# Sixteen added semaphore waits on GpSimd, ScalarE and VectorE in a four-layer convolution kernel

## The chip, the cores and the metric

The kernel runs on one core of a Trainium2 chip. Its time is device time in microseconds of the whole program. TensorE, VectorE, ScalarE and GpSimd (PE, DVE, ACT and POOL in the rows) each work through an instruction list of their own, in order; SyncE (SP) issues DMAs. They are kept in step by semaphores alone.

## The reference

The input is x, 16 images of 64 x 64 positions with 256 channels, float32. Four layers follow, each adding to x what it computes of the group-normed x (32 groups):

```
x = x + L0(gn(x))   # nearest of 1024 codes for each position: scores against the codebook, argmin, gather of the code
x = x + L1(gn(x))   # row attention: f, g (32 channels) and h (256) of x; sigmoid(f g^T) over the 64 columns; times h
x = x + L2(gn(x))   # per image: softmax over 4096 x 4096 outer products x0*x1, summed with x2, sigmoid, gates gn(x)
x = x + L3(gn(x))   # linear attention, 4 heads of 32: softmax of q and of k, context, output projection, layernorm
```

## The kernel before

An image is held channel-major in SBUF (`XT`: 2 halves of 128 channels by 4096 positions), two images at a time. Work goes in 8 groups `g` of 512 positions, `u` counts 128 positions in a group, `t = 4g + u`. Most scratch tiles have two halves, chosen by `g % 2`, so that group g writes where group g - 2 was read.

The steps of a group are functions that exist under one name on each engine that takes part. Layer 0 is `l0_norm` (ACT normalizes into `n_x`, rounds to `n_hi`; POOL makes the rest `n_lo`), `score` (PE), `best` and `index` (DVE), `index` (POOL: an indirect DMA gathers the code rows into `quant`), `turn0` (PE) and `add0` (DVE). Layer 1 is `l1_norm` (ACT, then POOL), `l1_fg` and `l1_h` (PE, then ACT and DVE), `l1_scores` (PE), `l1_tanh` (ACT), `l1_out` (PE, DVE). Layer 2 is `fill` (PE), `exp` (ACT), `sums` (PE), with `bexp`/`bsum` beside it and `gated`/`gating`/`gated_add` at its end. Layer 3 is `l3_norm`, `l3_k`, `l3_kexp`, `l3_kturn`, `l3_ctx`, `l3_qv`, `l3_q` and so on, then `combine`, `final_sq` and `final_out`. `gn` in three parts makes the scale and shift of a group norm.

Three images are in work at once: for each k, layers 0 and 1 of image k (`new`), layers 2 and 3 of image k - 1 (`old`) and the output of image k - 2 (`last`). The order in which each engine runs the steps is written out by hand, one list for each engine, for the first image, for the 15 rounds of the loop, and for the last.

A `Step` is a semaphore with a count for each image. `after(im, i)` is the value at which item i of image im is done. `room(im, i, d)` is the value at which the item d places before i is done, so that its buffer is free; such semaphores begin with a credit of d. `wait_ge` calls stand ahead of an instruction, in the order of the code. An instruction carries one wait itself; the waits beyond it stand in `EVENT_SEMAPHORE` instructions ahead of it, which the engine's sequencer handles and which have the line number of a `wait_ge`. For instance `l1_norm` on ACT waits at line 576 (`l1_hed`) and at line 577 (`l1_xn`) before its activation at line 578, and the trace has 128 such events with line 577.

Of the kernel before, what the change touches and what calls it, by code (L numbers as in the profile page):

```python
# [16 lines left out]
GT = 4  # L17
# [69 lines left out]
def build(nc, x, emb, emb_t, wfg, bfg, wh, bh, w3, b3, wqv, wk, w_out, b_out, gamma, beta, ident_in, gmat_in, out):  # L87
# [6 lines left out]
    with ExitStack() as ctx:  # L94
# [6 lines left out]
        def step(name, per=NG, depth=0):  # L101
# [140 lines left out]
        mean_ready, mean_ps, var_ready, var_ps, ve_ready, pow_done, gn_ready = (  # L242
            [step(f"{n}{l}", 1) for l in range(4)]
            for n in ("mean_ready", "mean_ps", "var_ready", "var_ps", "ve_ready", "pow_done", "gn_ready"))

        l0_xn, l0_hi, l0_lo = step("l0_xn"), step("l0_hi"), step("l0_lo", NG, 2)
        l0_scored, l0_maxed, l0_indexed = step("l0_scored", 2 * NT, 16), step("l0_maxed", 2 * NT, 2), step("l0_indexed", NT, 2)
        l0_turned, l0_added = step("l0_turned", 2 * NG, 4), step("l0_added", 2 * NG, 1)

        l1_xn, l1_hi, l1_lo = step("l1_xn"), step("l1_hi"), step("l1_lo", NG, 2)  # L250
# [160 lines left out]
        def _(pool):  # L411
# [19 lines left out]
            def l0_norm(im, g, part):  # L431
                if part < 3:
                    return
                pool.wait_ge(*l0_hi.after(im, g))
                nc.gpsimd.tensor_tensor(n_lo[:, g % 2, :, :], n_x[:, g % 2, :, :], n_hi[:, g % 2, :, :],  # L435
                                        ALU.subtract).then_inc(l0_lo.sem, 1)

            def index(im, t):
                g, u = t // GT, t % GT
                pool.wait_ge(*l0_indexed.after(im, t))  # L440
                nc.gpsimd.indirect_dma_start(  # L441
                    quant[:, g % 2, u, :], None, emb_t,
                    bass.IndirectOffsetOnAxis(ap=idx[:, t % (2 * GT), 0:1], axis=0),
                ).then_inc(gathered[g % 2][u], 16)

            def l1_norm(im, g):
                pool.wait_ge(*l1_hi.after(im, g))
                nc.gpsimd.tensor_tensor(n_lo[:, g % 2, :, :], n_x[:, g % 2, :, :], n_hi[:, g % 2, :, :],  # L448
                                        ALU.subtract).then_inc(l1_lo.sem, 1)

# [3 lines left out]
                nc.gpsimd.tensor_tensor(here, here, gated[:, g % 2, :, :], ALU.add).then_inc(g_added.sem, 1)  # L454

            def l3_norm(im, g):
                pool.wait_ge(*l3_hi.after(im, g))
                nc.gpsimd.tensor_tensor(o_lo[:, g % 2, :, :], o_x[g % 2], o_hi[:, g % 2, :, :],
                                        ALU.subtract).then_inc(l3_lo.sem, 1)
# [77 lines left out]
        def _(act):  # L537
# [31 lines left out]
                    last.then_inc(l0_hi.sem, 1)  # L569

            def l1_norm(im, g):
                act.wait_ge(*gn_ready[1].after(im))
                for k in range(KC):
                    last = normed(n_x[:, g % 2, k, :], im, k, g, 1)
                last.then_inc(l1_xn.sem, 1)
                act.wait_ge(*l1_hed.room(im, 2 * g + 1, 4))
                act.wait_ge(*l1_xn.after(im, g))
                nc.scalar.activation(n_hi[:, g % 2, :, :], n_x[:, g % 2, :, :], copy).then_inc(l1_hi.sem, 1)  # L578

            def l1_fg(im, g):  # L580
                act.wait_ge(*l1_fged.after(im, g))
                if im + g == 0:
                    act.wait_ge(weights_in, 16 * NW)
                for j, kept in enumerate((FT, GTm)):
                    rr = slice(2 * CK * j, 2 * CK * (j + 1))
                    last = nc.scalar.activation(kept[:, g % 2, :], PS[rr, 4, 0:2 * P], copy, bias=fg_bias[rr, 0:1])
                last.then_inc(l1_fgkept.sem, 1)

            def l1_tanh(im, g):
                act.wait_ge(*l1_scored.after(im, g))  # L590
                nc.scalar.activation(tanhs[:, g % 2, :], PS[:, 4, 0:GT * ROW], ACT.Tanh, scale=0.5).then_inc(l1_tanhed.sem, 1)
                act.wait_ge(*l1_tanhed.after(im, g))
                for r in range(2):
                    rr = slice(r * ROW, (r + 1) * ROW)
                    last = nc.scalar.activation(attn[rr, g % 2, :, rr], tanhs[rr, g % 2, :].rearrange("p (u i) -> p u i", u=GT),
                                                copy, bias=ones[rr, 0:1])
                last.then_inc(l1_attn.sem, 1)
# [55 lines left out]
                last.then_inc(g_normed.sem, 1)  # L653

            def l3_norm(im, g):
                act.wait_ge(*gn_ready[3].after(im))
                for k in range(KC):
                    last = normed(o_x[g % 2][:, k, :], im, k, g, 3)
                last.then_inc(l3_xn.sem, 1)
                act.wait_ge(*l3_qved.room(im, g, 2))  # L660
                act.wait_ge(*l3_xn.after(im, g))
                nc.scalar.activation(o_hi[:, g % 2, :, :], o_x[g % 2], copy).then_inc(l3_hi.sem, 1)

            def l3_kexp(im, g):
                act.wait_ge(*l3_kneg.after(im, g))
                nc.scalar.activation(ke[:, g % 2, :, :].rearrange("p u n -> p (u n)"), bank(0), ACT.Exp,
                                     bias=kneg[:, g:g + 1], accum_out=ksum[:, g:g + 1]).then_inc(l3_kexped.sem, 1)
# [141 lines left out]
        def _(dve):  # L809
# [40 lines left out]
            def gn(im, layer, part):  # L850
                q, b = layer // 3, gn_bank(layer)
                if part == 0:
                    dve.wait_ge(*stats_done[layer].after(im, NG - 1))
                    for k in range(KC):
                        link(v.bn_aggr(mv[:, q, k, :], stats[:, layer, k, :, :].rearrange("p g n -> p (g n)")))
                    if layer < 2:
                        v.tensor_copy(dm[:, q, :], mv[:, q, :, 0]).then_inc(mean_ready[layer].sem, 1)
                    else:
                        v.tensor_tensor(dm[:, q, :], mv[:, q, :, 0], beta_c[:, :], ALU.subtract).then_inc(mean_ready[layer].sem, 1)
                if part == 1:  # L860
                    dve.wait_ge(*mean_ps[layer].after(im))
                    if layer < 2:
                        v.tensor_copy(gm[:, q, :], PS[:, b, 0:KC])
                    else:
                        v.tensor_tensor(gm[:, q, :], PS[:, b, 0:KC], beta_c[:, :], ALU.add)
                    link(v.tensor_tensor(dm[:, q, :], dm[:, q, :], PS[:, b, 0:KC], ALU.subtract))
                    link(v.tensor_tensor(vv[:, q, :], dm[:, q, :], dm[:, q, :], ALU.mult))
                    v.tensor_tensor(vv[:, q, :], vv[:, q, :], mv[:, q, :, 1], ALU.add).then_inc(var_ready[layer].sem, 1)
                if part == 2:
                    dve.wait_ge(*var_ps[layer].after(im))  # L870
                    v.tensor_scalar(ve[:, q, :], PS[:, b, 4:4 + KC], GN_EPS, None, ALU.add).then_inc(ve_ready[layer].sem, 1)
                    dve.wait_ge(*pow_done[layer].after(im))
                    v.scalar_tensor_tensor(out=gt[:, layer, :], in0=gm[:, q, :], scalar=-1.0, in1=gs[:, layer, :], op0=ALU.mult,  # L873
                                           op1=ALU.mult).then_inc(gn_ready[layer].sem, 1)
# [37 lines left out]
                stat(im, g, 1)  # L912

            def l1_h(im, g, w):
                dve.wait_ge(*l1_hed.after(im, 2 * g + w))
                v.tensor_tensor(H[:, g % 2, 2 * w:2 * w + 2, :], bank(6 - w).rearrange("p (u n) -> p u n", u=2),
                                h_bias[:, :].unsqueeze(1).broadcast_to([P, 2, C]), ALU.add).then_inc(l1_hkept.sem, 1)
# [101 lines left out]
                                ALU.mult).then_inc(l3_qsoft.sem, 1)  # L1019

            def l3_kturn(im, g):
                dve.wait_ge(*l3_kturned.after(im, g))
                v.tensor_copy(kt[:, g % 2, :, :], bank(5).rearrange("p (u n) -> p u n", u=GT)).then_inc(l3_kback.sem, 1)

# [69 lines left out]
            def final_out(im, c):  # L1094
                g = c // 2
                dve.wait_ge(*f_rstd.after(im, g))
                if c % 2 == 0 and im * NG + g >= 2:
                    dve.wait_ge(stored[g % 2], 16 * (im * NG // 2 + g // 2))
                dve.wait_ge(*f_turned.after(im, c))
                for u in range(2 * (c % 2), 2 * (c % 2) + 2):  # L1100
                    last = v.scalar_tensor_tensor(out=yout[:, g % 2, u, :], in0=Y[:, g % 2, u, :],
                                                  scalar=rstd[:, g % 2, 1, u:u + 1], in1=PS[:, back_bank(im, c), u % 2 * C:(u % 2 + 1) * C],
                                                  op0=ALU.mult, op1=ALU.add)
                last.then_inc(f_half.sem, 1)
# [632 lines left out]
```

## Time and profile before

| | us, or a count |
|---|---|
| median of 3 runs | 5468.85 (5467.99 to 5471.41) |
| the profiled execution | 5467.99 |
| its span, first to last instruction | 5466.2 |
| instructions in its trace, events among them | 109580 |
| PE busy | 5123.3 (94%) |
| DVE busy | 4387.4 (80%) |
| ACT busy | 4037.1 (74%) |
| POOL busy | 1964.2 (36%) |

The span is what the rows cover; the time has 1.8 us more around it. A round of the loop takes about 328 us. Busy times leave out what the sequencers handle, such as the events. A line number is one of the kernel before; the changed kernel has the same instructions at lines up to 17 higher.

### The profile page before, as it was taken

Reading aid. Unit: us, or ns where it says so; the run is one execution under the profiler, and the core shown is the slowest. Engines: PE = TensorE matmul, PEld = TensorE weight load, DVE = VectorE, ACT = ScalarE, POOL = GpSimd, SP = SyncE. Lnnn points to the kernel's source line nnn. Section 1 sums busy time; section 2 is a strip of 40 time slices with the busy share of each in tenths; the row PEclk is TensorE's granted clock in tenths of the full one; section 3 lists DMA queues with packets and bytes.
Section 4 is the critical chain, followed back from the end, with each engine's and each line's share of the span. In section 5 each row is a group of like instructions: output and inputs, shape, how many; then the busy total and the mean of one; then the engine's idle time right before and its main releaser. Section 6 shows DMA issues by size and latency. Waiting matters only on the chain.

```text
span 5466.2 us, 109580 instructions
## 1 busy us (share of the span) xinstructions
PE 5123.3 (94%) x42984; PEld 2689.9 (49%) x42984; DVE 4387.4 (80%) x9218; ACT 4037.1 (74%) x6279; POOL 1964.2 (36%) x1594
## 2 busy tenths in 40 slices
PE   7799999999999999999999999999999999999986
PEld 3436445363543646445363553645446464453624
DVE  8478797887878888797887978778798887978836
ACT  1477878678786877868778786787868778786785
POOL 4225143342423425143351423424244351433403
PEclk9899999999999999999999999999999999999988
DMA  2010201102021020211102021020211102011000
GB/s 76 29 37 12 75 27 57 42 7 81 20 71 32 25 65 14 74 29 44 52 8 80 22 67 36 21 66 17 71 32 37 56 11 77 26 62 38 12 31 32
DMA packets 167966, 227.84 MB, mean 42 GB/s; under 512 B 13793, under 2 KB 146657, under 8 KB 167457
## 3 DMA queue, kind: packets, MB, share of 16 engines
q1 hardware_dynamic: 142880, 153.70, 8.5%
q0 software_dynamic: 24576, 67.14, 4.2%
q8 instruction: 345, 5.65, 0.4%
q14 instruction: 165, 1.34, 0.1%
HBM read 153.55 MB, written 67.24 MB: 40 GB/s over the span
## 4 chain that ended last, share of the span: by engine, by line
PE 72%; DVE 13%; ACT 9%; issue 4%; DMA 1%; POOL 1%; DVEq 0%; SPq 0%; ACTq 0%; POOLq 0%
PE PS L1239 36%; PE PS L1416 14%; PE PS L1407 5%; PE PS L1350 3%; PE PS L1515 2%; PE PS L1273 2%; ACT big L618 2%; DVE work L896 2%; PE PS L1297 2%; DVE stats L878 2%; ACT n_x L551 2%; PE PS L1316 1%; DVE idx L902 1%; PE PS L1365 1%; ACT soft L618 1%
## 5 line engine op out<-in xcount | busy, mean ns | idle before, releaser
L618 ACT ACTIVATE big<-PS 128x1024 f32<-128x1024 f32 x1216 | 1207.5, 1028 | 384.7 <-PE PS L1407 350.8
L441 POOL DMA_INDIRECT quant_H<-emb_t,idx x512 | 509.0, 994 | 906.2 <-DVE idx L902 879.7
L1239 PE MATMUL PS<-e_hi,n_hi 128*128 128x512 f16 x2048 | 780.4, 381 | 16.5 <-DVE m L896 9.0
L1239 PE MATMUL PS<-e_lo,n_hi 128*128 128x512 f16 x2048 | 777.2, 379 | 0.0
L1239 PE MATMUL PS<-e_hi,n_lo 128*128 128x512 f16 x2048 | 777.2, 379 | 0.0
L618 ACT ACTIVATE soft<-PS 128x1024 f32<-128x1024 f32 x576 | 577.3, 1030 | 257.8 <-PE PS L1407 255.8
L1416 PE MATMUL PS<-big,w 128*4 128x512 f32 x4864 | 680.3, 646 | 0.0
L878 DVE BATCH_NORM_STATS2 stats<-XT 128x6 f32<-128x512 f32 x1024 | 652.9, 683 | 11.0 <-POOL XT L454 1.0
L902 DVE FIND_INDEX8 idx<-m,work 128x8 uint32<-128x1024 f32 x512 | 624.2, 1219 | 0.0
L1407 PE MATMUL PS<-rhs,lhs 12*128 12x512 bf16 x3584 | 522.8, 403 | 71.5 <-ACT big L618 35.6
L495 POOL TENSOR_TENSOR rstd<-rstd,mhalf 128x4 f32<-128x4 f32 x128 | 131.9, 1030 | 1123.1 <-DVE rstd L1091 1123.1
L896 DVE CUSTOM_DVE_ANT_0 work<-PS,e_bias 128x512 f32<-128x512 f32 x512 | 350.6, 685 | 163.7 <-PE PS L1239 162.5
L1407 PEld LDWEIGHTS PS<-rhs,lhs 12*128 12x128 bf16 x3584 | 126.8, 91 | 677.9 <-ACT big L618 242.2
L551 ACT ACTIVATE n_x<-XT,gt,gs 128x512 f32<-128x512 f32 x512 | 393.6, 806 | 72.9 <-DVE gt L873 70.5
L896 DVE CUSTOM_DVE_ANT_0 work<-PS,e_bias,m 128x512 f32<-128x512 f32 x512 | 379.4, 741 | 32.0 <-PE PS L1239 26.7
L1239 PE MATMUL PS<-qv_hi,o_both 128*128 128x256 f16 x2048 | 357.9, 273 | 21.6 <-DVE soft L1032 21.6
L1239 PEld LDWEIGHTS PS<-e_hi,n_hi 128*128 128x128 f16 x2048 | 199.4, 97 | 351.1 <-DVE m L896 123.8
L435 POOL TENSOR_TENSOR n_lo<-n_x,n_hi 128x1024 f16<-128x1024 f32 x128 | 273.6, 2137 | 259.3 <-ACT n_hi L567 258.2
L992 DVE CUSTOM_DVE_ANT_0 o_x<-o_x,o_both 128x1024 f32<-128x1024 f32 x256 | 311.5, 1217 | 61.8 <-ACT o_x L629 61.8
L454 POOL TENSOR_TENSOR XT<-XT,big 128x1024 f32<-128x1024 f32 x128 | 303.5, 2379 | 151.8 <-DVE big L999 149.9
L629 ACT ACTIVATE o_x<-o_both,negm,s 128x1024 f32<-128x1024 f32 x256 | 317.7, 1241 | 38.7 <-DVE bnum L992 38.7
L448 POOL TENSOR_TENSOR n_lo<-n_x,n_hi 128x1024 f16<-128x1024 f32 x128 | 273.4, 2136 | 160.7 <-ACT n_hi L578 160.7
(214 smaller groups left out, 11030.5 us busy)
## 6 DMA issues: line engine op xcount, KB each, us to landing
xin<-x SPq DMA_DIRECT2D x128, 512.0 KB, 4.3
out<-yout SPq DMA_DIRECT2D x128, 512.0 KB, 3.0
o_both<-rows_d SPq DMA_DIRECT2D x32, 512.0 KB, 7.1
quant_H<-emb_t,idx POOLq DMA_INDIRECT x512, 2.8
XT<-emb SPq DMA_DIRECT2D x1, 1024.0 KB, 6.1
rows_d<-n_hi SPq DMA_DIRECT2D x32, 4.0 KB
XT<-wh SPq DMA_DIRECT2D x1, 256.0 KB, 5.5
XT<-wqv SPq DMA_DIRECT2D x1, 256.0 KB, 5.6
```

The costliest lines, as they stand in the source:

```text
L441: nc.gpsimd.indirect_dma_start(quant[:, g % 2, u, :], None, emb_t, bass.IndirectOffsetOnAxis(ap=idx[:, t % (2 * GT), 0:1], axis=0),).then_ ...
L454: nc.gpsimd.tensor_tensor(here, here, gated[:, g % 2, :, :], ALU.add).then_inc(g_added.sem, 1)
L551: return nc.scalar.activation(dst, XT[:, im % 2, k, g, :], copy, scale=gs[:, layer, k:k + 1], bias=gt[:, layer, k:k + 1])
L618: nc.scalar.activation(E[h % 3][:, z * 1024:(z + 1) * 1024], bank(2 * z, 2), ACT.Exp).then_inc(exped.sem, 1)
L629: nc.scalar.activation(EB, x0_row, ACT.Exp, scale=s3[:, 1, t:t + 1], bias=negm[:, t:t + 1], accum_out=bden[:, i:i + 1]).then_inc(b_exped.s ...
L878: last = v.bn_stats(stats[:, layer, k, g, :], XT[:, im % 2, k, g, :])
L896: v.tensor_tensor_reduce(biased[:, t % 2, part], bank(5 + half), e_bias[:, part], 1.0, m8[:, t % 2, 0:1] if half else -BIG, ALU.add, ALU.m ...
L902: v.max_index(idx[:, t % (2 * GT), :], m8[:, t % 2, :], biased[:, t % 2, :]).then_inc(l0_indexed.sem, 1)
L992: v.tensor_tensor_reduce(EB, EB, x2_row, 1.0, 0.0, ALU.mult, ALU.add, bnum[:, i:i + 1]).then_inc(b_summed.sem, 1)
L1239: ins = mm(dst, a, b, start=first and j == 0, stop=last and j == 2)
L1407: ins = mm(bank(r), lhs[rr, t * P:(t + 1) * P], rhs[rr, f * GW:(f + 1) * GW], start=True, stop=True)
L1416: ins = mm(PS[32 * q:32 * q + 4, 4, :], w2[:, t, f, :], E[h % 3][:, q * 512:(q + 1) * 512], start=h == 0, stop=h == HALVES - 1, skip_group ...
```

## The change

Waits are added ahead of instructions that are there already: each names the last reader (or writer) of the buffer half that the instruction is about to overwrite (or read). No instruction other than waits is added, removed or moved.

```diff
@@ POOL
             def l0_norm(im, g, part):
+                pool.wait_ge(*l0_scored.room(im, 2 * (g * GT + GT) - 1, 4 * GT))
                 pool.wait_ge(*l0_hi.after(im, g))
             def index(im, t):
+                pool.wait_ge(*l0_turned.room(im, t // 2, 4))
                 pool.wait_ge(*l0_indexed.after(im, t))
             def l1_norm(im, g):
+                pool.wait_ge(*l1_hed.room(im, 2 * g + 1, 4))
                 pool.wait_ge(*l1_hi.after(im, g))
+                if g > 1:
+                    pool.wait_ge(*l1_fged.after(im, g - 2))
             def l3_norm(im, g):
+                pool.wait_ge(*l3_qved.room(im, g, 2))
                 pool.wait_ge(*l3_hi.after(im, g))
@@ ACT
             def l1_norm(im, g):
+                act.wait_ge(*l1_lo.room(im, g, 2))
                 act.wait_ge(*gn_ready[1].after(im))
 ...
                 act.wait_ge(*l1_hed.room(im, 2 * g + 1, 4))
+                if g > 1:
+                    act.wait_ge(*l1_fged.after(im, g - 2))
                 act.wait_ge(*l1_xn.after(im, g))
             def l1_fg(im, g):
+                act.wait_ge(*l1_scored.room(im, g, 2))
                 act.wait_ge(*l1_fged.after(im, g))
             def l1_tanh(im, g):
+                act.wait_ge(*l1_outed.room(im, 2 * g + 1, 4))
                 act.wait_ge(*l1_scored.after(im, g))
             def l3_norm(im, g):
+                act.wait_ge(*l3_lo.room(im, g, 2))
                 act.wait_ge(*gn_ready[3].after(im))
             def l3_kexp(im, g):
+                act.wait_ge(*l3_kturned.room(im, g, 2))
                 act.wait_ge(*l3_kneg.after(im, g))
@@ DVE
             def gn(im, layer, part):   # part 1
                     dve.wait_ge(*mean_ps[layer].after(im))
+                    dve.wait_ge(*mean_ready[layer].after(im))
             def l1_h(im, g, w):
+                dve.wait_ge(*l1_outed.room(im, 2 * g + 1, 4))
                 dve.wait_ge(*l1_hed.after(im, 2 * g + w))
             def l3_kturn(im, g):
+                dve.wait_ge(*l3_ctxed.room(im, g, 2))
                 dve.wait_ge(*l3_kturned.after(im, g))
             def final_out(im, c):
                 dve.wait_ge(*f_rstd.after(im, g))
+                dve.wait_ge(*f_y.after(im, c))
```

ScalarE in layer 1 of a round of the loop, before (L578 rounds to `n_hi`, L591 is the tanh of `l1_tanh`, L586 the first copy of `l1_fg`):

```order
L578 ACTIVATE n_hi<-n_x 128x1024 [waits l1_xn,l1_hed]
L591 ACTIVATE work<-PS 128x256 [waits l1_scored]
L595 ACTIVATE attn<-work,ones 64x4x64 [waits l1_tanhed]
L595 ACTIVATE attn<-work,ones 64x4x64
L551 ACTIVATE o_x<-XT,gt,gs 128x512 [waits g_gated]
L586 ACTIVATE work<-PS,fg_bias 64x256 [waits l1_fged]
L586 ACTIVATE work<-PS,fg_bias 64x256
L551 ACTIVATE n_x<-XT,gt,gs 128x512 [waits gn_ready1]
```

The same place now:

```order
L587 ACTIVATE n_hi<-n_x 128x1024 [waits l1_xn,l1_fged,l1_hed]
L602 ACTIVATE work<-PS 128x256 [waits l1_scored,l1_outed]
L606 ACTIVATE attn<-work,ones 64x4x64 [waits l1_tanhed]
L606 ACTIVATE attn<-work,ones 64x4x64
L557 ACTIVATE o_x<-XT,gt,gs 128x512 [waits g_gated]
L596 ACTIVATE work<-PS,fg_bias 64x256 [waits l1_fged,l1_scored]
L596 ACTIVATE work<-PS,fg_bias 64x256
L557 ACTIVATE n_x<-XT,gt,gs 128x512 [waits gn_ready1,l1_lo]
```

Nothing has moved; four of the five waiting instructions of the layer have one wait more. GpSimd at the start of layer 0 of a round, before:

```order
L428 TENSOR_TENSOR gs<-ve,mhalf 128x2 [waits ve_ready0]
L435 TENSOR_TENSOR n_lo<-n_x,n_hi 128x1024 [waits l0_hi] x2
L441 DMA quant_H<-emb_t,idx 128x256 [waits l0_indexed] x4
L435 TENSOR_TENSOR n_lo<-n_x,n_hi 128x1024 [waits l0_hi]
L441 DMA quant_H<-emb_t,idx 128x256 [waits l0_indexed] x6
```

The same place now:

```order
L428 TENSOR_TENSOR gs<-ve,mhalf 128x2 [waits ve_ready0]
L436 TENSOR_TENSOR n_lo<-n_x,n_hi 128x1024 [waits l0_hi,l0_scored] x2
L443 DMA quant_H<-emb_t,idx 128x256 [waits l0_indexed,l0_turned] x4
L436 TENSOR_TENSOR n_lo<-n_x,n_hi 128x1024 [waits l0_hi,l0_scored]
L443 DMA quant_H<-emb_t,idx 128x256 [waits l0_indexed,l0_turned] x6
```

Here too every step has kept its place, and the one wait of each has become two.

## Rows read from the trace of the kernel before

**Rows 1.** The page: shares of the chain that ended last.
```profile
PE 72%; DVE 13%; ACT 9%; issue 4%; DMA 1%; POOL 1%; DVEq 0%; SPq 0%; ACTq 0%; POOLq 0%
```

**Rows 2.** Stretches of one round: length, busy PE, PEld, DVE, ACT, POOL, clock, DMA.
```profile
774.00:834.00 60.00, 55.22 (x665) 41.44 (x665) 49.74 (x91) 52.88 (x82) 37.09 (x18) 0.97 0.01 4
1000.00:1104.00 104.00, 103.85 (x618) 42.73 (x620) 100.00 (x217) 63.33 (x81) 41.79 (x35) 1.00 0.13 38
```

**Rows 3.** Events by line: count, duration ns min/median/max, first and last start.
```profile
L577 ACTq EVENT_SEMAPHORE  x128: 17/17/17, 161.8 to 5114.5; - x128
L617 ACTq EVENT_SEMAPHORE  x15: 38/38/38, 569.1 to 5190.8; - x15
L998 DVEq EVENT_SEMAPHORE  x128: 49/50/514, 457.9 to 5359.3; - x128
```

**Rows 4.** Chain of waits in the last image: start us, us, what.
```profile
5374.27 0.07 issue
5374.34 2.13 POOL o_both L458
...
5383.04 0.02 issue
5383.06 0.02 ACTq L671
5383.08 0.04 issue
5383.12 0.61 ACT xin L672
5383.73 0.03 issue
5383.76 0.02 DVEq L1027
5383.78 0.04 issue
5383.82 0.70 DVE qmx L1030
```

**Rows 5.** Timeline of the set-up: start us, us, what, idle before it.
```profile
17.42 0.61 ACT L548 ACTIVATE h_hi<-XT 128x512 f16<-128x512 f32 x1
18.18 0.43 POOL L421 TENSOR_TENSOR fg_lo<-XT,fg_hi 128x128 f16<-128x128 f32 x1 [2.10 <-ACT h_hi L548]
```

**Rows 6.** Timeline of ScalarE in layer 2.
```profile
932.20 1.96 ACT L618 ACTIVATE soft<-PS 128x1024 f32<-128x1024 f32 x2
934.09 2.10 ACT L618 ACTIVATE big<-PS 128x1024 f32<-128x1024 f32 x2
```

**Rows 7.** Timeline of the entry to layer 1.
```profile
785.01 2.13 POOL L448 TENSOR_TENSOR n_lo<-n_x,n_hi 128x1024 f16<-128x1024 f32 x1 [2.97 <-ACT n_hi L578]
787.24 0.29 PE L1316 MATMUL PS<-n_hi,fg_hi 128*32 128x256 f16 x4 [0.83 <-issue]
```

**Rows 8.** Who waited for whom: us in total, times, longest us.
```profile
ACT soft L666 <- DVE kneg L1008: 101.6, 32, 4.3
ACT n_x L551 <- DVE gt L873: 70.5, 17, 39.0
PEld PS L1515 <- DVE yout L1101: 40.0, 66, 1.3
DVE quant_H L916 <- PE PS L1239: 34.3, 46, 9.2
ACT work L591 <- PE PS L1340: 28.9, 36, 3.1
ACT work L586 <- PE PS L1316: 17.5, 19, 1.3
```

**Rows 9.** Line 916, who waited for it (us, times).
```profile
  PE PS L1350: 4.5, 14
```

**Rows 10.** Line 1297, what ended its idle time (us, times).
```profile
  DMA quant_H<-emb_t,idx: 17.8, 27
```

## The prediction

> **What bounds the kernel now.** First the shares of the chain that ended last: the reader is to see PE with 72%, and the three engines that get new waits with 13%, 9% and 1% [rows 1]. So TensorE sets the time, and a delay elsewhere counts only where PE, or the engine that PE then waits for, stands still for it. Second, the stretches of a round: in layer 0 beside layer 2 (1000 to 1104 us) PE is busy for 103.85 of 104.00 us, so that nearly every new stall of PE lengthens the program; where layer 1 stands beside the end of layer 2 (774 to 834 us) PE is busy for 55.22 and ACT for 52.88 of 60.00 us [rows 2], so the two hand the chain to each other. Third, the list of who waited for whom, which shows how often an instruction that gets a new wait now starts late, released by another engine [rows 8].
>
> **Do the new waits block?** Each names work that has already ended when the older wait passes, because every engine runs in order. POOL's `l0_norm` waits for scores that ACT has waited for before the `n_hi` that POOL reads. `index` waits for a `turn0` whose sum DVE's list has (`add0(t // 2 - 4)`) ahead of `index(t)`. ACT's `l1_tanh` waits for `l1_out(g - 2)`, which PE's list has ahead of `l1_scores(g)`; the same is true of `l1_h(g)`, of `l3_k(g)` after `l3_kturn(g - 2)` and of `l3_kturn(g)` after `l3_ctx(g - 2)`. `l1_lo` and `l3_lo` of group g - 2 were waited for by the PE work that ACT's older steps wait for. `f_y` and `mean_ready` are DVE's own, and the answers of POOL and PE that DVE waits for come after them. So nothing is held until a later moment than today, and no transfer is triggered earlier or later but by the small delays below. What is left is the price of the wait instruction itself.
>
> **What is added.** An instruction carries its first wait, and an event takes up to two more. By the code's order the older wait, the one that comes last in time, stands behind the new one in 11 of the 16 places and is pushed into the event, while the instruction keeps the new one, long satisfied. On POOL one wait becomes two or three for `l0_norm`, `l1_norm`, `l3_norm` at 128 each and for `index` at 512: 896 events. ACT gets 128 x 5 less 1 = 639 (`l1_norm`'s first, `l1_fg`, `l1_tanh`, `l3_norm`, `l3_kexp`; one `l1_fg` has an event already). DVE gets 64 (`gn`) + 256 (`l1_h`) + 128 (`l3_kturn`) + 126 (`final_out`, where a store is waited for) = 574. In `gn` the late wait stays on the instruction. Elsewhere an event grows from one wait to two: ACT's `n_hi` of line 578 96 times, `final_out` 130 times.
>
> **The price of one.** Where the event holds the late wait, the chain shows 0.02 us until the event starts, 0.02 for it and 0.04 until ACT's instruction starts; for DVE 0.03, 0.02 and 0.04 [rows 4]. The delay over a wait that the instruction carries is the last two, 0.06 us on ACT; for DVE I take 0.07, since these are rounded. On POOL a carried wait starts 0.07 us after the release [rows 4]; in the set-up, with an event, POOL's line 421 starts at 18.18 after ACT ended at 17.42 + 0.61 = 18.03, which is 0.15 [rows 5]: 0.08 more. An event with two waits takes 38 ns on ACT against 17, and on DVE 50 [rows 3] against 0.02 us [rows 4]: 0.02 and 0.03 more. Where the event's waits are satisfied while the instruction before still runs, it costs nothing: the first of two exponentials at 934.09 has an event (line 615) and starts before the pair ahead of it has ended at 932.20 + 1.96 = 934.16 [rows 6].
>
> **The sum**, over the places where a release comes late and PE stands behind it:
> - Entry to layer 1. PE idles 0.83 us and starts at 787.24, 0.10 after POOL's `n_lo` ended (785.01 + 2.13) [rows 7]; that hangs on ACT's L551, released late by `gt` 17 times [rows 8]. ACT 0.06 + POOL 0.08 = 0.14, in 16 images: 2.2 us. Queued behind the waiting instructions are ACT's next norm and POOL's next `n_lo`, which shift alike.
> - Middle of layer 1: L591 was released late by PE 36 times [rows 8]. Between nothing (PE has other work) and 36 x 0.06 = 2.2; I take one per round, 15 x 0.06 = 0.9, since ACT is busy for most of the stretch and its events are passed early. L586 was late 19 times and L666 32 times [rows 8], 1.1 and 1.9 at most; I take nothing, as PE has other steps queued between.
> - `l1_h`: DVE was late 46 times [rows 8], and PE waited for it 14 times [rows 9]: 14 x 0.07 = 1.0, between nothing and 3.2.
> - Gathers: PE waited for a gather 27 times [rows 10]. Each is issued 0.08 us later: 27 x 0.08 = 2.2. The trace has no gather behind an event, so this may be anything from nothing to twice that, 4.3. Queued behind each on POOL are the next gathers and `n_lo`; POOL is busy for 41.79 of 104 us there [rows 2].
> - Events with two waits: line 577 waits for ACT's own instruction just before and is always late, 96 x 0.02 = 1.9; about half stands on the path, 1.0. `final_out`: PE's loads waited for L1101 66 times [rows 8], half of them of the kind that grows: 33 x 0.03 = 1.0, at most 130 x 0.03 = 3.9.
> - Layer 3 is entered behind other PE work but in the last image: 0.1. `gn` and `l3_kturn`: nothing.
>
> 2.2 + 0.9 + 1.0 + 2.2 + 1.0 + 1.0 + 0.1 = 8.4 us. The profiled execution took 5467.99, so 5476.4; it lies 0.9 below the median of the runs, so 5477.3, or 0.15% more. The floor is no delay at all. The ceiling has every late release on the path: ACT 104 x 0.06 = 6.2, DVE 3.2, POOL 16 x 0.08 + 4.3 = 5.6, double waits 1.9 + 3.9, together 20.8: 5489.7. Below nothing there is no bound to set, since no wait is taken away and no order changes.
>
> **Rivals.**
> - *Absorbed* (5466 to 5472). The 0.06 to 0.08 us pass into idle time that a later wait would have had anyway. For it: PE has some 5 us of idle time in the 60 us of layer 1 [rows 2]. Against it: in layer 0 PE has 0.15 us of it in 104.
> - *Satisfied events cost too, slower* (5490 and more). The place is ACT in layer 1: 8 groups with 3 new events each, 24 in a round. If the sequencer could not pass them under the instruction before, each would cost the 0.06 of a late one: 15 x 24 x 0.06 = 21.6 us, and the time would be 5468.9 + 21.6 + 8.4 = 5498.9; it decides from about one in two of them exposed. Against it: the exponentials with an event start without a gap [rows 6]. The Trainium skill, Advanced Engine Details and Errata, section Network/Comms, gives 50 to 100 ns for a sequencer to read a semaphore's value; paid at each of these 360 events, that would be an estimated 18 to 36 us. By that rule alone this rival would be the likeliest; the trace agrees with its size only for late releases, and shows it hidden otherwise.
> - *One of the waits does block.* If ACT's norm of group g had to stay behind POOL's queue, each time it could cost one `n_lo`, 2.13 us [rows 7]; once a round gives 15 x 2.13 = 32 us, 5501. The orders of the lists speak against it.
>
> **How the numbers follow.** Two runs of this kernel can be told apart from about 0.2%, 10.9 us, so slower means above 5479.8 and faster below 5457.9. The forecast has 0.66: its own range is 5472 to 5488, of which 0.17 lies above 5479.8. Absorbed 0.22, satisfied events 0.07, a blocking wait 0.03. For a gain nothing speaks but a luckier meeting of queues, 0.02. So faster 0.02, same 0.49 + 0.22 = 0.71, slower 0.17 + 0.07 + 0.03 = 0.27. The range 5467 to 5488 leaves out the two dear cases and little more.
>
> **What would show it.** The trace has 109580 instructions and should have 2109 more, all events. In each image the first ACT norm of layer 1 should start 0.06 us later after `gt`, the first `n_lo` 0.15 after `n_hi` in place of 0.07, and PE's idle time before L1316 should grow by 0.14. Busy times of the engines should stay within 0.1%; layer 2 up to the start of the next layer 0, where only `final_out` has a new wait, should keep its length. The forecast is wrong if ACT shows gaps of 0.06 us between instructions that nobody releases late, if POOL's gathers move by more than 0.1 us, or if a new wait's semaphore comes after the older one. The Trainium skill, Perfetto Trace Analysis, section DVE / Act Engine Instruction, says that the sequencer is free for the next instruction once it has pushed one into the wait queue, whereas one that only the sequencer handles holds it until its wait is over: what is queued behind a late event is then decoded late as well. By that, short instructions behind a late event would show gaps too; no row here prices that.

## The result: 0.78% slower, outside the range

| | before | after |
|---|---|---|
| median of the runs, us | 5470.13 (5467.99 to 5473.2) | 5508.83 (5506.09 to 5519.77) |
| profiled execution, us (span) | 5467.99 (5466.2) | 5509.96 (5508.2) |
| mean granted clock in it | 0.963 | 0.957 |
| instructions in the trace | 109580 | 111689 |

The ratio is 1.0078, interval 1.0062 to 1.0092. I had 5477.3 and a range up to 5488. The 2109 additional events are there to the one. The time is not where my sum looked for it.

### The profile page after: what moved, and what is told of

It is laid out like the page before. It is cut to its first block, busy times and chain, and to the rows that moved or that the text cites. A ratio compares the mean times of both kernels' runs of the same rounds, so it can differ in the third digit from the quotient of the medians.

```text
span 5508.2 us, 111689 instructions
## 1 busy us (share of the span) xinstructions
PE 5155.3 (94%) x42984; PEld 2694.4 (49%) x42984; DVE 4393.6 (80%) x9218; ACT 4042.8 (73%) x6279; POOL 1977.0 (36%) x1594
## 4 chain that ended last, share of the span: by engine, by line
PE 72%; DVE 12%; ACT 7%; issue 5%; DMA 1%; POOL 1%; DVEq 0%; SPq 0%; ACTq 0%; POOLq 0%
PE PS L1256 36%; PE PS L1433 13%; PE PS L1424 6%; PE PS L1367 3%; PE PS L1532 2%; DVE work L910 2%; PE PS L1290 2%; ACT big L629 2%; PE PS L1314 2%; DVE idx L916 1%; DMA quant_H<-emb_t,idx 1%; PE PS L1333 1%; ACT n_x L557 1%; DVE stats L892 1%; PE PS L1382 1%
## 5 line engine op out<-in xcount | busy, mean ns | idle before, releaser
L443 POOL DMA_INDIRECT quant_H<-emb_t,idx x512 | 521.6, 1019 | 929.0 <-DVE idx L916 768.4
L436 POOL TENSOR_TENSOR n_lo<-n_x,n_hi 128x1024 f16<-128x1024 f32 x128 | 273.6, 2137 | 240.9 <-ACT n_hi L573 188.0
L1433 PE MATMUL PS<-soft,w 128*4 128x512 f32 x2304 | 336.0, 658 | 0.0
```

The costliest lines, as they stand in the source:

```text
L443: nc.gpsimd.indirect_dma_start(quant[:, g % 2, u, :], None, emb_t, bass.IndirectOffsetOnAxis(ap=idx[:, t % (2 * GT), 0:1], axis=0),).then_ ...
L1433: ins = mm(PS[32 * q:32 * q + 4, 4, :], w2[:, t, f, :], E[h % 3][:, q * 512:(q + 1) * 512], start=h == 0, stop=h == HALVES - 1, skip_group ...
```

## The profile after

The page first: busy time of the engines after, and the shares of its chain.

```profile
PE 5155.3 (94%) x42984; PEld 2694.4 (49%) x42984; DVE 4393.6 (80%) x9218; ACT 4042.8 (73%) x6279; POOL 1977.0 (36%) x1594
PE 72%; DVE 12%; ACT 7%; issue 5%; DMA 1%; POOL 1%; DVEq 0%; SPq 0%; ACTq 0%; POOLq 0%
```

The line of before that answers to the first:

```profile
PE 5123.3 (94%) x42984; PEld 2689.9 (49%) x42984; DVE 4387.4 (80%) x9218; ACT 4037.1 (74%) x6279; POOL 1964.2 (36%) x1594
```

The shares hardly differ from [rows 1], and DVE, ACT and POOL are busy for 6, 6 and 13 us more. PE runs the same 42984 matmuls and is busy for 32.0 us more, while its idle time grows from 5466.2 - 5123.3 = 342.9 to 352.9, by 10.0. So of the 42 us 10 are more waiting and 32 are the same matmuls taking longer, and the clock does most of that. A mean clock of 0.957 means 2 x (1 - 0.957) x 5508 = 474 us at the lower of the two levels (1.2 GHz), against 2 x 0.037 x 5466 = 404 before. The trace's own list of clock stretches says 473.8 and 404.3, and PE is busy in 82 to 84% of them. At half speed PE works 0.41 us longer in each us of them: 69.5 x 0.41 = 28 of the 32.

That is not yet what the clock costs the program, because a slower PE also waits less for the others. The net price shows where one kernel is run many times, as its half clock differs from run to run. The 55 executions of the kernel before beside the experiments have between 382 and 483 us of it, and take 0.26 us more for each us more. Over all 153 executions listed for the 14 kernels, each set about its own mean, it is 0.28 (0.26 to 0.31). At 0.28 the 69.5 us are worth 19 of the 42, and some 23 are delay. Against the mean of before in the first group of experiments, the eight executions of after are 36 us longer with 45 us more half clock: 12.5 for the clock and 23.4 for delay.

**The waiting** is at the gathers. First after, then before: a search of codes on DVE and the gather on POOL that it releases (start us, us, what, idle before).

```profile
739.65 1.22 DVE L916 FIND_INDEX8 idx<-m,work 128x8 uint32<-128x1024 f32 x1
741.64 0.95 POOL L443 DMA_INDIRECT quant_H<-emb_t,idx  x1 [3.55 <-DVE idx L916]
```

```profile
743.14 1.22 DVE L902 FIND_INDEX8 idx<-m,work 128x8 uint32<-128x1024 f32 x1
744.63 0.95 POOL L441 DMA_INDIRECT quant_H<-emb_t,idx  x1 [3.05 <-DVE idx L902]
```

The search ends at 740.87 and the gather starts 0.77 us later; before, 744.36 and 0.27. By the semaphore events of the whole trace it is 762 ns (407 gathers within 10 ns of it) against 259 (424). The event itself is short (count, ns min/median/max, first and last start):

```profile
L442 POOLq EVENT_SEMAPHORE  x512: 17/17/17, 49.0 to 5097.6; - x171
```

On a tensor_tensor of POOL a late event adds 65 ns (68 to 133), by the same semaphore events. A gather behind one loses 0.50 us, over seven times as much. I read the rest as preparation of the gather that runs under the wait when the gather carries it, and starts only afterwards when an event ahead of it waits; no row shows that preparation by itself. In the chain after, that half us stands as "issue" between the search and the DMA:

```profile
767.97 1.31 DVE idx L916 x2
769.32 0.72 issue
770.04 2.75 DMA quant_H<-emb_t,idx
772.79 0.04 issue
772.83 0.45 PE PS L1314 x2
```

Who waited for it, from the list of waits after (us, times, longest), and under it what ended the idle time before line 1314, which answers to [rows 10]:

```profile
PEld PS L1314 <- DMA quant_H<-emb_t,idx: 23.5, 28, 2.6
PE PS L1314 <- DMA quant_H<-emb_t,idx: 16.6, 21, 2.2
```

```profile
  DMA quant_H<-emb_t,idx: 40.2, 49
```

The first of the two lists before:

```profile
PEld PS L1297 <- DMA quant_H<-emb_t,idx: 11.9, 20, 2.2
PE PS L1297 <- DMA quant_H<-emb_t,idx: 6.0, 7, 2.0
```

The 27 waits of [rows 10] were 20 of weight loads, which run beside the matmuls, and 7 of PE itself. Now PE waits 21 times, for 16.6 us in place of 6.0: 10.6 us. That its whole idle time grew by 10.0 is chance: in the trace of the first kernel below these waits grow by 9.9 us and the idle time by 2.7, since other waits shrink.

**Does the new wait block?** The profile names PE's line 1314 as the releaser of 23 gathers after, for 53.7 us, which looks like it. The semaphore events say no: for every one of the 512 gathers `l0_turned` had its value before `l0_indexed` did, the closest by 15 us. A gather carries the new, satisfied wait, and the page reads its releaser from there.

**The rest of my list.** The entry to layer 1 after:

```profile
779.16 0.16 DVE L887 SCALAR_TENSOR_TENSOR gt<-gm,gs 128x2 f32<-128x2 f32 x1 [0.84 <-POOL gs L428]
779.41 1.52 ACT L557 ACTIVATE n_x<-XT,gt,gs 128x512 f32<-128x512 f32 x2 [0.99 <-DVE gt L887]
781.02 1.06 ACT L587 ACTIVATE n_hi<-n_x 128x1024 f16<-128x1024 f32 x1
782.22 2.13 POOL L453 TENSOR_TENSOR n_lo<-n_x,n_hi 128x1024 f16<-128x1024 f32 x1 [3.10 <-ACT n_hi L587]
```

0.09 us behind `gt` and 0.14 behind `n_hi`, as forecast. What ended PE's idle time before the line of the first products of layer 1 (us, times) was this before

```profile
  issue: 33.6, 74
  ACT work L591: 30.3, 76
  POOL n_lo L448: 6.3, 1
```

and is this after:

```profile
  ACT work L602: 35.8, 76
  issue: 29.6, 71
  POOL n_lo L453: 6.7, 1
```

Together 70.2 us and 72.1, over all groups of the layer. Ahead of the first product of each image, where my sum had 2.2 us, it did not grow: 13.4 us over the 16 images before, with none at all in five of them, and 11.6 after. The start is later, but the wait it should lengthen is not there every time. The waits at other edited steps hardly moved (to compare with [rows 8]), and all 256 events of `final_out` now take the 50 ns of a double one [rows 3]:

```profile
ACT soft L679 <- DVE kneg L1023: 103.9, 32, 4.7
PEld PS L1532 <- DVE yout L1118: 40.7, 66, 1.3
DVE quant_H L931 <- PE PS L1256: 36.7, 51, 9.4
ACT work L602 <- PE PS L1357: 30.3, 36, 3.1
```

```profile
L1116 DVEq EVENT_SEMAPHORE  x256: 49/50/50, 584.4 to 5500.8; - x128
```

**The clock.** Stretches at the entry to layer 2 (length, busy PE, PEld, DVE, ACT, POOL, clock, DMA): after,

```profile
892.00:896.00 4.00, 2.53 (x47) 1.42 (x45) 3.83 (x8) 3.26 (x6) 0.00 (x0) 1.00 0.00 0
896.00:903.00 7.00, 6.79 (x64) 1.88 (x62) 4.43 (x18) 5.21 (x8) 0.00 (x0) 0.51 0.36 102
```

and the same place before:

```profile
893.00:897.00 4.00, 2.57 (x49) 1.67 (x46) 3.87 (x7) 2.91 (x6) 0.00 (x0) 1.00 0.00 0
897.00:904.00 7.00, 6.14 (x74) 1.84 (x76) 4.99 (x21) 7.00 (x10) 0.00 (x0) 1.00 0.41 132
```

Both have PE busy for only some 2.55 of 4 us, for two pauses of 0.7 us each. After it the clock is at half for 7 us in the one, at full in the other, and PE gets through 64 matmuls in place of 74. Such a pause doesn't always bring the fall, but in both traces each round has three places where it can: the entry to layer 2, `gn` of layer 0 and `gn` of layer 1. Half clock by place in rounds 1 to 14, us, from the trace's list:

| | entry to layer 2 | gn 0 | gn 1 | first and last image |
|---|---|---|---|---|
| before | 68 | 102 | 68 | 165 |
| after | 102 | 116 | 79 | 177 |

The windows of [rows 2] show it too. Layer 1 has 0.94 for 0.97, and in layer 0 PE waits 1.1 us for two gathers, where it waited for none:

```profile
1000.00:1104.00 104.00, 102.90 (x606) 42.51 (x602) 98.73 (x216) 62.62 (x81) 42.58 (x35) 1.00 0.14 39
774.00:834.00 60.00, 55.27 (x664) 41.78 (x661) 48.31 (x88) 52.52 (x82) 37.11 (x18) 0.94 0.01 2
```

## The experiments

Each is compared with runs of the kernel before on its own chip. Clock is the mean over the runs; half clock is 2 x (1 - clock) x time; the next column, called the delay below, is the mean time less 0.28 of it, against the same for before, with the standard error of the kernel's own mean. For the kernels with matmuls, which have some 240 us less of half clock, it hangs on that price: their own executions give 0.34, which would add 14 us. What they differ by among themselves hardly depends on it. The ratios, with their 95% intervals, differ a little from those of the medians (1.0048 and 1.0049 for the first two); differences in us below are of means unless they are said to be of medians. PE's waits for gathers, us, are from the list of waits of the profiled run.

| kernel | median, us | ratio, interval | clock | half clock | delay: time less 0.28 of it, against before | PE waits for gathers |
|---|---|---|---|---|---|---|
| before, beside the next four | 5474.9 | | 0.9603 | 435 | 0 +- 0.5 | 6.0 |
| gather's wait alone | 5501.1 | 1.0040 (1.0025 to 1.0055) | 0.9567 | 477 | +12.8 +- 1.7 | 15.9 |
| all but it | 5501.8 | 1.0041 (1.0026 to 1.0057) | 0.9563 | 480 | +12.2 +- 0.7 | 3.7 |
| gather's wait behind | 5480.0 | 1.0004 (0.9994 to 1.0015) | 0.9602 | 436 | +1.6 +- 0.5 | 4.2 |
| all waits behind | 5485.0 | 1.0012 (1.0002 to 1.0022) | 0.9586 | 454 | +2.7 +- 0.6 | 3.6 |
| before, beside the next four | 5474.5 | | 0.9603 | 435 | 0 +- 0.6 | |
| late waits first | 5472.1 | 0.9992 (0.9983 to 1.0001) | 0.9594 | 445 | -6.2 +- 0.4 | |
| layer 3's waits alone | 5484.9 | 1.0014 (1.0004 to 1.0023) | 0.9590 | 450 | +4.7 +- 0.8 | |
| before with matmuls | 5436.9 | 0.9924 (0.9911 to 0.9938) | 0.9822 | 194 | +29.5 +- 1.0 | 4.6 |
| after with matmuls | 5457.0 | 0.9963 (0.9949 to 0.9976) | 0.9832 | 183 | +52.3 +- 0.5 | 16.4 |
| before, beside the last four | 5478.3 | | 0.9599 | 439 | 0 +- 0.8 | |
| matmuls, late waits first | 5420.0 | 0.9901 (0.9883 to 0.9919) | 0.9832 | 182 | +18.0 +- 1.1 | |
| half the matmuls, late first | 5442.9 | 0.9932 (0.9912 to 0.9951) | 0.9760 | 261 | +13.2 +- 1.6 | |
| matmuls and gather's wait | 5448.6 | 0.9948 (0.9933 to 0.9964) | 0.9817 | 200 | +39.8 +- 1.2 | 17.1 |
| matmuls at layer 2 alone | 5447.8 | 0.9943 (0.9930 to 0.9955) | 0.9698 | 329 | -0.3 +- 0.8 | |

The expectations were written with 0.41 as the price of a us at half clock. At that price kernels 1, 2 and 5 have delays of +7.4, +6.2 and -7.5 us, and these are the figures that the later expectations start from.

**1. The gather's wait alone.**

```
 def index(im, t):
     g, u = t // GT, t % GT
+    pool.wait_ge(*l0_turned.room(im, t // 2, 4))
     pool.wait_ge(*l0_indexed.after(im, t))
```

> The kernel before with one new wait alone: index waits for the room of l0_turned ahead of its own l0_indexed, so that the late wait sits in an event and the gather carries the satisfied one. Theory G (an indirect gather starts 0.26 us after a release that it carries and 0.76 behind a late event, and the 0.50 us are exposed in layer 0): most of the 39 us, so 5495 to 5505 us, with the gathers at 0.76 again. Rival R (the rest of the waits, 0.06 to 0.11 us at each late release on ACT, DVE and POOL, make the loss): within 10 us of before, 5470 to 5480, though the gathers start at 0.76. Rival C (any disturbance of PE's rhythm costs through stretches at the lower clock): something between, with PE's stretches at half clock as long as in the changed kernel (472 us, before 403).

The median lies in G's 5495 to 5505, but before is at 5474.9 here. The edit costs 25 us (26 by medians), neither G's most of 39 nor under R's 10. Its gathers start 762 ns after their release, PE waits 15.9 us for them, and 12.8 us are delay. 42 us more of half clock make the other 12, so C is in it.

**2. All but it.**

```
 def index(im, t):
     g, u = t // GT, t % GT
-    pool.wait_ge(*l0_turned.room(im, t // 2, 4))
     pool.wait_ge(*l0_indexed.after(im, t))
```

> The changed kernel without index's new wait: 1597 of the 2109 new events stay. Theory G: what my sum had without the gathers, 6 us, so 5474 to 5480 us, and gathers at 0.26 us after their release. Rival R: 5495 to 5508, since the waits that it blames are all in. Rival C: more than 5485 with stretches at half clock near 472 us.

G's 5474 to 5480 is missed by 22 us, and G as the whole story falls; R's range is met here and C's condition too. The delay is 12.2 us, twice what my sum had without the gathers (8.4 - 2.2 = 6.2); the clock adds 46 x 0.28 = 13. The two halves together give 0.40 + 0.41 = 0.81% for the whole's 0.78%. Their delays add up, 12.8 + 12.2 = 25.0 for the whole's 23.4; their half clock doesn't, 42 + 46 us for 45.

**3 and 4. The same events behind the late wait.** In 3 the two waits of `index` change places; in 4 the same is done in all 11 steps where a new wait stood first, as here:

```
 def l1_fg(im, g):
-    act.wait_ge(*l1_scored.room(im, g, 2))
     act.wait_ge(*l1_fged.after(im, g))
+    act.wait_ge(*l1_scored.room(im, g, 2))
```

> As the first of these, but the new wait stands behind l0_indexed: 512 new events all the same, each now with the satisfied wait, while the gather carries the late one. Theory G: 0 to 3 us over before (5469 to 5473 us), gathers at 0.26 us. Rival S (an event costs its time wherever it stands): as slow as the first one, 5495 or more. Rival C: over 5480.

> The changed kernel with the same 2109 events, but in each of the 11 steps where the older wait stood behind a new one the older stands first, so that the instruction carries the wait that comes late. Theory G and the small delays of late events alike: 0 to 4 us over before (5469 to 5474 us), with releases to starts as before (ACT 23 ns, DVE 24, POOL 68, gathers 260). Rival S: 5500 or more. Rival C: over 5480.

Delays of 1.6 and 2.7 us: 512 or 2109 satisfied events cost next to nothing (S falls). The fourth still has the events with two waits, for which my sum had 2.0 us. The late wait on the instruction gives the old latencies back (ACT 23 ns, DVE 24, POOL 68, gathers 259), and PE waits 4.2 and 3.6 us for gathers. So nearly all of the delay, and most of the loss, is the order of two lines in each step. The fourth still has 0.0017 less clock, worth 5 us, and lies 8 us over before (10 by medians): my 0 to 4 us was too low, and C's bound of 5480 was passed.

**5. Late waits first, in before.** Five old steps get the same treatment, the largest being `best`:

```
 def best(im, t, half):
     part = slice(half * 512, (half + 1) * 512)
+    dve.wait_ge(*l0_scored.after(im, 2 * t + half))
     if half == 0:
         dve.wait_ge(*l0_indexed.room(im, t, 2))
     else:
         dve.wait_ge(*l0_maxed.after(im, 2 * t))
-    dve.wait_ge(*l0_scored.after(im, 2 * t + half))
```

> The kernel before with no new wait: in five steps that already had two or three (best, gating, final_sq, final_out on DVE, l3_qv on ACT) the one that comes late stands first, so that the instruction carries it. Releases that cost 94 to 133 ns before should cost 24. Theory K (a late release that PE stands behind costs its delay and then, through longer pauses, more time at the lower clock): 5 to 25 us faster than before, with a granted clock above 0.961. Rival D (only the delay counts, and DVE's are off PE's path): within 3 us of before. Rival S (an order of waits is worth nothing): no change and releases as before.

The releases that took 94 to 133 ns take 24, but for the second half of `best`, whose wait for its own first half now stands in the event (134 ns). The delay falls by 6.2 us. The clock takes 3 of it back (its trace has 137 us of half clock at the entry to layer 2, before 68), and the interval reaches 1.0001. The time alone, 2 us less by medians, would also suit D. K's sign for the clock is wrong here: shorter delays did not raise it.

**6 and 7. PE kept busy in the pauses.** The edit is cut to its lines with `keep`; in the first round, which has no `last`, the first of them has no wait.

```
+def keep(im, n, b, *done):
+    if done:
+        pe.wait_ge(*done)
+    for _ in range(n):
+        mm(PS[:, b, 256:384], ident16[:, :], ident16[:, :], start=True, stop=True)
...
-fill(old, 30, 1); gn(new, 0, 1); fill(old, 31, 0)
-gn(new, 0, 2); fill(old, 31, 1)
+keep(last, 5, 5, *f_y.after(last, 2 * NG - 1))
+fill(old, 30, 1); keep(old, 4, 5); gn(new, 0, 1); fill(old, 31, 0)
+keep(old, 5, 5); gn(new, 0, 2); fill(old, 31, 1)
...
-fill(old, 55, 0); gn(new, 1, 1); fill(old, 55, 1); gn(new, 1, 2)
-sums(old, 53); sums(old, 54); sums(old, 55); gate_chain(old, 0); l1_fg(new, 0)
+keep(new, 14, 5, *l0_maxed.after(new, 2 * NT - 2))
+fill(old, 55, 0); keep(new, 4, 5); gn(new, 1, 1); fill(old, 55, 1); keep(new, 5, 5); gn(new, 1, 2)
+sums(old, 53); sums(old, 54); sums(old, 55); keep(new, 9, 5); gate_chain(old, 0)
+keep(new, 11, 5); l1_fg(new, 0)
...
+keep(new, 9, 7, *pieces_kept[1].after(new, 1))
```

> The kernel before with 57 additional matmuls of 128 columns in each round (some 3.4 us of PE work at full clock), in the places where PE stands idle ahead of the stretches at half clock: around gn of layers 0 and 1, ahead of the first products of layer 1, and ahead of layer 2. They write a free bank and nobody reads them. Theory K (the stretches at half clock follow from these pauses, and each us of them costs about 0.4): fewer of them, 250 to 350 us in place of some 430, and 20 to 70 us faster. Rival P (the clock doesn't hang on these pauses, or the matmuls come late and delay the work behind them): half clock as before, and 0 to 50 us slower.

> The changed kernel with the same additional matmuls in the same places. Theory K: two thirds of its loss is clock, so it comes within 15 us of the kernel before with these matmuls, what is left being the delays of 13 us. Rival D (the loss is all delay): it stays 38 us above the kernel before with these matmuls. Rival P: above 5508.

The count in the first expectation is wrong: there are 66 in a round, 990 in all. PE is busy with them for 79.1 us, 0.08 us each and not the 0.1 of the later expectations. They take 241 us of half clock away, more than K had. At 0.28 that is worth 68 us, against some 30 that the matmuls add, and the kernel is 38 us faster than before. Its mean clock, and under it the windows of the entry to layer 2 and, in two rows, of `gn` of layer 0:

```profile
core 0: 5437.6 us, clock 0.982
```

```profile
890.00:900.00 10.00, 8.99 (x126) 3.30 (x120) 7.38 (x26) 9.62 (x13) 0.00 (x0) 1.00 0.43 140
965.00:975.00 10.00, 9.16 (x74) 3.28 (x74) 6.75 (x19) 9.66 (x13) 0.69 (x1) 1.00 0.16 54
975.00:985.00 10.00, 8.44 (x58) 2.62 (x55) 2.99 (x8) 9.46 (x14) 2.13 (x1) 1.00 0.00 0
```

`gn` of layer 0 in before, where the clock falls:

```profile
970.00:980.00 10.00, 8.44 (x55) 2.74 (x58) 6.71 (x19) 9.49 (x13) 0.70 (x1) 0.91 0.16 54
980.00:990.00 10.00, 10.00 (x58) 2.34 (x51) 2.28 (x6) 8.90 (x12) 2.14 (x1) 0.75 0.00 0
```

The change costs 20 us with the clock held in both, and 36 to 39 without. K's "within 15" is missed by 5, because its two thirds of clock rest on the price of 0.41. The delay between the two is 52.3 - 29.5 = 22.8 us, as large as without the matmuls (23.4): the delay is the larger part of the loss, and the matmuls take away the clock's part.

**8. Layer 3's waits alone.**

```
+pool.wait_ge(*l3_qved.room(im, g, 2))      # l3_norm, ahead of l3_hi
+act.wait_ge(*l3_lo.room(im, g, 2))         # l3_norm, ahead of gn_ready[3]
+act.wait_ge(*l3_kturned.room(im, g, 2))    # l3_kexp, ahead of l3_kneg
+dve.wait_ge(*l3_ctxed.room(im, g, 2))      # l3_kturn, ahead of l3_kturned
```

> The kernel before with the new waits of layer 3 alone: l3_norm on POOL and ACT, l3_kexp, l3_kturn (512 events). My sum had 0.1 us for them. Theory K: they delay the end of layer 3, where PE's pauses stand ahead of layer 2, so the stretches at half clock that start there (7 of 15 rounds before, 11 after) come in more rounds: 5 to 15 us slower, nearly all of it clock. Rival L (the entry to layer 1 and l1_h carry what the gathers don't): within 3 us of before.

0.14% slower, 8.8 us: 4.7 of delay, and 4 for 15 us more of half clock, so not "nearly all" clock; in its trace the entry to layer 2 has 109 us of it in 12 rounds (before 68 in 8). L falls, and so does my 0.1 us for layer 3.

**9 to 12. What the matmuls hold, and where.** The first is 5 and 6 together; the second has 35 of the 66 matmuls; the third is 6 with the edit of 1; the fourth has only the last line of the edit of 6.

> The kernel before with both: the late waits first, and all 66 additional matmuls in each round (990 in all; 66, not 57 as I wrote for the first kernel with them, some 0.1 us each in its trace). Alone, the order of the waits took 7.5 us from the time without the clock's share and gave most of it back in clock. Theory K: with the clock held by the matmuls the 7 us stay, so 5428 to 5434 us, 5 to 9 below the kernel with the matmuls alone. Rival D (nothing is gained from the order in either case): 5434 to 5440.

> As the one above with 35 of the 66 matmuls in each round, in the same nine places. They save 31 x 15 x 0.1 = 47 us of PE work, of which a third or so lay in PE's waits anyway. Theory K: where the shorter ones still keep the clock up it gains up to 25 us on the full set (5405 to 5430); where a pause is left too long the clock falls there again, and it lands between 5430 and 5450. Told apart by the half clock in the trace: under 250 us or over 300.

> The kernel before with the 66 matmuls and index's new wait alone ahead of l0_indexed. Without the matmuls that wait cost 7 us of delay and 17 us of clock. Theory K: the clock's share is gone, the delay stays: 5 to 15 us over the kernel with the matmuls (5442 to 5452). Rival D (delay of gathers is all of it): 24 us or more over it, 5461 or more.

> The kernel before with the 9 matmuls ahead of layer 2 alone, and none around gn. Theory K says place by place: the stretches at half clock that start at the entry to layer 2 (7 of 15 rounds in the trace before) go, those around gn of layers 0 and 1 (two in each round, 10 us together) stay; half clock 330 to 400 us, time 0 to 20 us below before, the clock's gain less 15 x 9 x 0.1 = 13 us of work of which two thirds lie in PE's waits. Rival A (any added work holds the clock up everywhere): below 300 us of half clock.

Kernels 5 and 6 ran beside other runs of before than these four, so each is compared by its own. The first kernel is the fastest of all, 1.0% under before, and 8 us better than K's 5428. The late waits first bring it 0.0023 of the ratio of kernel 6, 13 us, and 11.5 us of delay, where they took 6.2 off before; D falls. The gather's wait has a delay of 10.3 us over kernel 6, where it was 12.8 without the matmuls, and of the clock's 12 us some 2 are left, as K had it. Half the matmuls are too few: 261 us of half clock, between K's two marks, 89 of the 277 in the trace at the entry to layer 2, and 23 us slower by medians than the full set (17 by means). The fourth tells the places apart. Half clock in its trace is 17 us at the entry to layer 2, 92 at `gn` 0 and 61 at `gn` 1 (before 68, 102, 68). The pause that was filled lost three quarters of its share, the other two a tenth. Its time is 31 us under before where I expected at most 20: 110 us of half clock at 0.28, with nothing left for the 135 matmuls.

## Why the prediction was wrong

- **Right.** 2109 events, no wait that blocks, satisfied events nearly free, late ones 0.06 us dearer on ACT and 0.07 on DVE and POOL, and the later starts at the entry to layer 1. The change adds 15 waits, not the 16 that the title and the prediction count; the 11 places and the 2109 are right.
- **The gathers' term was mis-sized, and so was its bound.** "Each is issued 0.08 us later: 27 x 0.08 = 2.2", "anything from nothing to twice that, 4.3". A gather starts 0.50 us later, and the 27 waits became 49, PE's own 21 in place of 7, for 10.6 us more. The edit alone has a delay of 12.8 +- 1.7 us, 10.3 with the matmuls. I had priced a DMA's issue by a tensor_tensor's row and taken "twice" as the end of the range. The trace had a row against it: a gather starts 0.27 us after its release and a tensor_tensor 0.07, so a gather's start does more work, and nothing said that this stays hidden behind an event.
- **The other delays were too small by half.** I had 6.2 us for all but the gathers, and kernel 2 has 12.2 +- 0.7. The step that shows it best is layer 3, which I entered with 0.1 us and which has 4.7 in kernel 8. The 2.2 us at the entry to layer 1 came from one image, and the idle time there did not grow. How the rest divides among the steps no run shows.
- **The sum had no term for the clock.** It let PE's matmuls take what they took, with a granted clock of 0.963. The same matmuls took 32.0 us longer at 0.957, and the program lost some 12 to 19 us by it, a third to a half of the loss. The forecast's "ceiling has every late release on the path", 20.8 us, lies under the delays alone, 23 us, and the clock comes on top.
- **The sign I gave right, the odds wrong.** 0.27 for slower came from delays only. The row that speaks of the clock stood in the page (0.97 in the stretch of layer 1 [rows 2]) and I read it only for busy times.
- **The rival of satisfied events falls** with kernels 3 and 4, 512 and 2109 of them for delays of 1.6 and 2.7 us. The Trainium skill's 50 to 100 ns for a read of a semaphore (Advanced Engine Details and Errata, section Network/Comms) fits the size of late events here (60 to 70 ns more), and no satisfied one.
- **My last sentences had the mechanism and no price.** Work behind a late event does start late: 0.50 us for a gather, 0.06 to 0.07 for the engines' own work. The Trainium skill, Perfetto Trace Analysis, section Sequencer-only Instruction (DRAIN, etc), has the sequencer ready for the next instruction only after such an instruction has waited and run; by that rule the trace agrees, and for a DMA that rule should have widened my range.

What stays open: why a delay changes how often the clock falls at one of these pauses. Kernels 1, 2 and 8 had more half clock with more delay, but kernel 5 had more with less, the half clock of kernels 1 and 2 does not add up to the whole's, and two traces with the same pause differ. The clock's share of one edit is therefore not to be forecast from its delay. That most of it goes when the pause is filled is shown, place by place, in the trace of kernel 12. The price of 0.28 comes from how time and half clock vary together, and no run sets the clock by itself.

## What to carry to other kernels

When an instruction has several waits, write the one that will come last first, so that the instruction carries it, above all on a DMA issued by POOL. An additional wait that is long satisfied costs next to nothing behind it (1.6 us for 512). And where PE bounds a kernel, put the clock in the sum: compare busy time at an equal count of matmuls, and look at the pauses of PE before counting nanoseconds; here 5.3 us a round of matmuls that nobody reads bought more than any order of waits. A us at the lower clock costs the program less than PE's busy time says (0.28 for 0.41 here); repeated runs of one kernel give the price.

## What the runs showed of the hardware that I had not expected

- An indirect gather on POOL starts 259 ns after a release that it carries and 762 behind a late event; tensor_tensor goes from 68 to 133, ACT from 23 to 83, DVE from 24 to 94, and 122 with two waits in the event.
- Half clock is a large account of its own: 435 us of some 5476 in before, 182 with the pauses filled. 990 matmuls that nobody reads, 79.1 us of busy PE, made the kernel 38 us faster.
- Where an instruction carries a satisfied wait and an event the late one, the profile may name the satisfied one's engine as the releaser (PE for 23 gathers, 53.7 us).
